# The openings of the first attention: tokens by way of a DRAM copy, another order of SP's transfers, and banks in one turn

## The reference, cut to what matters

```python
# L0: 32 query heads of 16, 8 key/value heads, post layer norm
q = x @ Wq + bq;  k = ctx @ Wk + bk;  v = ctx @ Wv + bv
attn = softmax(q k^T / sqrt(16) + mask)           # four query heads share one key head
x = layernorm(attn v @ Wo + bo + x) * gamma + beta
# L1: two attentions (16 heads of 128, pre layer norm, one learned key and value more) and an MLP
x = x + attention(layernorm(x), ctx; wq1 ...);  x = x + attention(layernorm(x), ctx; wq2 ...)
x = x + gelu(layernorm(x) @ w_fc1 + b_fc1) @ w_fc2 + b_fc2
```

## Time and profile before

| what | us |
|---|---|
| runs before (three) | 2495.45, 2500.95, 2508.18; median 2500.95 |
| the profiled execution, its own time | 2500.87 |
| its span, first to last instruction | 2499.0 |
| busy: PE / DVE / ACT / POOL | 2319.4 / 1397.6 / 996.5 / 786.4 |
| DMA | 248.60 MB, mean 99 GB/s |

### The profile page before, as it was taken

One profiled execution on the slowest core, in us unless ns is written; L12 is line 12 of the kernel. 1 busy time (PEld: TensorE's weight loads), 2 busy tenths in 40 slices (PEclk: granted clock), 3 DMA queues, 4 the chain that ended last, 5 costly groups with the idle time before them and its releaser, 6 DMA issues. The chain is left out here.

```text
span 2499.0 us, 36057 instructions
## 1 busy us (share of the span) xinstructions
PE 2319.4 (93%) x13176; PEld 2074.8 (83%) x13176; DVE 1397.6 (56%) x3138; ACT 996.5 (40%) x2191; POOL 786.4 (31%) x847
## 2 busy tenths in 40 slices
PE   6698899999999999998988979999999999999988
PEld 5576789998989999997776758898999899998976
DVE  4697544454565455456538965454545654455564
ACT  3596433242433333243128953243434333242420
POOL 4132322415141422414541332415141422415055
PEclk8899999999999999999998999999999999999999
DMA  8341223233323323234363213223332323233222
GB/s 254 100 133 44 85 86 110 81 89 119 97 83 95 94 86 110 81 89 138 118 191 101 76 39 101 85 85 119 94 96 86 94 86 110 81 91 117 81 71 80
DMA packets 136996, 248.60 MB, mean 99 GB/s; under 512 B 35663, under 2 KB 57295, under 8 KB 135799
## 3 DMA queue, kind: packets, MB, share of 16 engines
q1 hardware_dynamic: 93327, 123.54, 16.7%
q10 hardware_dynamic: 43496, 122.76, 16.0%
HBM read 221.35 MB, written 27.65 MB: 100 GB/s over the span
## 5 line engine op out<-in xcount | busy, mean ns | idle before, releaser
L622 POOL TENSOR_SCALAR wk_hi<-raw 128x512 fp32r<-128x512 f32 (+1 forms) x84 | 53.6, 638 | 905.4 <-DMA raw<-in_wk 751.1
L1325 ACT ACTIVATE probs<-scores,prm 112x376 f32<-112x376 f32 x256 | 147.0, 575 | 342.5 <-DVE prm L1682 342.4
L755 PE MATMUL pj_two<-ctx_hi,wk_hi 128*128 128x376 f32 x736 | 253.0, 344 | 10.6 <-POOL wk_lo L624 4.6
L756 PE MATMUL pj_two<-ctx_lo,wk_hi 128*128 128x376 f32 x736 | 248.3, 337 | 0.0
L757 PE MATMUL pj_two<-ctx_hi,wk_lo 128*128 128x376 f32 x736 | 247.6, 336 | 0.0
L1466 DVE TENSOR_TENSOR rr<-pj_two,rr 128x448 fp32r<-128x448 f32 (+2 forms) x200 | 132.8, 665 | 163.2 <-ACT rr L1102 163.1
L624 POOL TENSOR_TENSOR wb_lo<-raw,wb_hi 128x512 fp32r<-128x512 f32 x152 | 200.4, 1318 | 12.7
L1468 DVE SCALAR_TENSOR_TENSOR k_lo<-pj_two,cur,k_hi 128x375 fp32r<-128x375 f32 x172 | 104.4, 607 | 169.7 <-ACT k_hi L1104 169.7
L1104 ACT ACTIVATE k_hi<-pj_two,cur 128x375 fp32r<-128x375 f32 x172 | 98.6, 573 | 247.6 <-PE pj_two L757 242.7
L760 PE MATMUL tp_two<-ident,probs 112*126 112x112 f32 (+1 forms) x1152 | 163.8, 267 | 33.8 <-ACT probs L1245 18.2
L760 PEld LDWEIGHTS tp_two<-ident,probs 112*126 112x126 f32 (+1 forms) x1152 | 146.2, 160 | 56.3 <-ACT probs L1245 18.8
(11 more groups left out here) (246 smaller groups left out, 6640.1 us busy)
## 6 DMA issues: line engine op xcount, KB each, us to landing
nat<-nat_scratch ACTq DMA_DIRECT2D x256, 384.0 KB, 3.7
raw<-in_wq SPq DMA_DIRECT2D x72, 256.0 KB, 3.2
raw<-in_wo SPq DMA_DIRECT2D x72, 256.0 KB, 2.6
raw<-in_wk SPq DMA_DIRECT2D x64, 256.0 KB, 3.8
raw<-in_wv SPq DMA_DIRECT2D x64, 256.0 KB, 4.1
raw<-in_w SPq DMA_DIRECT2D x64, 256.0 KB, 2.9
nat_scratch<-rr ACTq DMA_DIRECT2D x7, 1536.0 KB, 6.8
qo<-queries_scratch SPq DMA_DIRECT2D x128, 56.0 KB, 2.4
```

The source lines that it names most:

```text
L622: nc.gpsimd.tensor_scalar(hi, src, 1.0, 0.0, ALU.mult, ALU.add).then_inc(split_hi, 1)
L755: nc.tensor.matmul(dst, l_hi, r_hi, start=first, stop=False)
L756: nc.tensor.matmul(dst, l_hi, r_lo, start=False, stop=False)
L1325: nc.scalar.activation(probs[0:L, h, 0:SK], scores[n % SCR][0:L, 0:SK], ACT.Exp, bias=neg_max[0:L, h:h + 1], accum_out=row_sum[0:L, h:h + ...
```

## The change

- **Tokens.** A DRAM scratch `x_copy` is new. SP copies each half's columns of `x_t` into it by one transfer (`copy_x`: the first half's ahead of all but the key weights, the second's in L0's attention), and loads them by two transfers of 448 KB into `pt_hi` and `pt_lo` (`x_came`, `load_x`). ScalarE casts the high part into `h_hi`, VectorE subtracts into `h_lo` (`split_x`). For the second half this is done in the last step of the first half's MLP.
- **Key weights.** GpSimd writes the scaled high part by one instruction; VectorE makes the low part from the raw slot and frees the slot (`wk0_rest`).
- **qo** is cleared first of all in the first half, and after the last chunk of `wq0` in the second.
- **Order of units.** The split of a context (`c`) and of the tokens (`x`) are named in the order; n3 comes after v0, and other units move (`pre_order`).
- **SP.** The stores of queries stand among the others in both openings, the queries of chunk 0 are loaded by 4 transfers in place of 16, the loads of bias rows and the zeros of `bx` move.
- **Banks.** `padded` goes; unit n of the whole program uses bank n modulo 3.

```diff
-def padded(n):
-    return -(-n // PJ) * PJ
+def pre_order(half):
     if half == 0:
-        order = "n0 n1 k0 k1 n2 n3 q0 k2 vt0 k3 vt1 v0 q1 vt2 v1 q2 vt3 v2 q3 v3"
+        order = "c0 n0 c1 k0 n1 k1 c2 n2 vt0 x0 k2 q0 vt1 v0 c3 n3 q1 vt2 v1 k3 q2 vt3 v2 q3 v3"
     else:
-        order = "k0 q0 k1 vt0 q1 vt1 v0 k2 q2 vt2 v1 k3 q3 vt3 v2 v3"
+        order = "k0 q0 k1 q1 vt0 q2 vt1 v0 k2 q3 vt2 v1 k3 vt3 v2 v3"
...
-    at["l0"], mid["l0"] = at["pre"] + padded(len(PRE[half])), mid["pre"] + len(PRE[half])
+    at["l0"], mid["l0"] = at["pre"] + len(PRE[half]), mid["pre"] + len(PRE[half])
...
+                def load_x(half):
+
+                    sp.wait_ge(x_copied, half * 16 + 16)
+                    for i in range(2):
+                        sp.dma_start(x_came[i], x_dram[2 * i * P:2 * (i + 1) * P, half * T:(half + 1) * T].rearrange(
+                            "(c p) n -> p c n", p=P)).then_inc(x_t_in, 16)
+
+                def copy_x(half):
+                    cols = slice(half * T, (half + 1) * T)
+                    sp.dma_start(x_dram[:, cols], x_t[:, cols]).then_inc(x_copied, 16)
...
+                if hf == 0:
+                    copy_x(0)
                 load_q0(base + RAW_Q0, 0)
-                for c in range(DC - 1):
-                    load_x(c)
+                load_v0(0)
+                if hf == 0:
+                    load_x(0)
+                load_v0(1)
                 if hf == 0:
                     store_keys0(0, *pre_split("k", 0))
-                load_x(DC - 1)
-                if hf == 0:
                     sp.dma_start(rows8_dram[0], bias_v).then_inc(rows8_in, 16)
                     sp.dma_start(rows8_dram[1], bv).then_inc(rows8_in, 16)
                     store_keys0(1, *pre_split("k", 1))
+                    load_q0(base + RAW_Q, 1)
+                    load_keys0(0, 0)
+                    load_keys0(0, 1)
+
+                    sp.wait_ge(pj_free, pre_freed("n", 2, SC - 1) + PJ)
+                    load_mask()
+                    load_q0(base + RAW_Q + 1, 2)
+                    store_keys0(2, *pre_split("k", 2))
+                    store_queries0(0, *pre_split("q", 0))
+                    load_q0(base + RAW_Q + 2, 3)
+                    load_queries0(0, 0)
+                    load_keys0(0, 2)
+                    sp.wait_ge(rows8_in, 32)
...
+                    store_queries0(1, *pre_split("q", 1))
+                    store_keys0(3, *pre_split("k", 3))
+                    store_queries0(2, *pre_split("q", 2))
+                    load_keys0(0, 3)
+                    store_queries0(3, *pre_split("q", 3))
+                else:
+                    for c in range(1, C0):
+                        load_q0(base + RAW_Q + c - 1, c)
                     store_keys0(0, *pre_split("k", 0))
...
+                            copy_x(1)
...
+                    sp.wait_ge(pj_ready, gpj + unit["r", HB - 1, DC - 1] + 1)
+                    sp.wait_ge(ex_in, 16 + NG * HB * 48)
+                    sp.sem_inc(sp_passed, 1)
+                    load_x(1)
...
+                    nc.gpsimd.tensor_scalar(hi, src, SCALE0, 0.0, ALU.mult, ALU.add).then_inc(split_hi, 1)
...
+            def split_x(half):
+                act.wait_ge(x_t_in, (half + 1) * 32)
+                for i in range(2):
+                    nc.scalar.activation(h_hi[:, 2 * i:2 * i + 2, :], x_came[i], ACT.Copy).then_inc(tok_hi, 1)
...
+            def wk0_rest(half):
+
+                for i in range(2):
+                    src, hi, lo = wk0_pieces(i)
+                    dve.wait_ge(split_hi, half * RAW_H + i + 1)
+                    nc.vector.scalar_tensor_tensor(lo, src, SCALE0, hi.bitcast(F32), ALU.mult,
+                                                   ALU.subtract).then_inc(w_ready["k"], 2)
+                    dve.wait_ge(w_ready["k"], half * WK_H * DC + 2 * (i + 1))
+                    dve.sem_inc(raw_free[i], 1)
...
-                    move(k_hi[:, h, 0:S], pj[unit % PJ][:, 0:S], pj_ready, gpj + unit + 1,
+                    move(k_hi[:, h, 0:S], pj[(gpj + unit) % PJ][:, 0:S], pj_ready, gpj + unit + 1,
```

More of the change, by code:

```diff
@@ L70, in pre_units, with banked @@
     return names
+def banked(names):
+    return [n for n in names if n[0] not in ("c", "x")]
+def pre_units(half):
+    return banked(pre_order(half))
 def pre_mids(half):
     names, held = [], None
-    for name in pre_units(half):
+    for name in pre_order(half):
         if name[0] == "vt" and name[1] > 0:
@@ L789, in out_part @@
                         ready(h)
-                    last = three(pj[unit % PJ][0:L, :],
+                    last = three(pj[(base + unit) % PJ][0:L, :],
                                  [s[:, h, b * L:(b + 1) * L] for s in src],
```

219 lines of the change are left out of this document (108 added, 111 removed).

## The result

The changed kernel takes 2487.42 us (median of 7 runs, 2484.52 to 2488.33), the kernel before 2504.41 us beside it (7 runs). The ratio is 0.9935, interval 0.9921 to 0.9949: faster by 0.65%. The profiled spans are 2499.0 and 2484.3 us, so 14.7 us are gone where 30 were forecast (17.0 by the two medians); the time lies inside the range.

What follows compares the result with a forecast made beforehand. SP's in-order queue, sending the last query stores late, was taken to set the end of both L0 openings; 18 us in the first plus 12 in the second off 2500.87 gave 2471 us, range 2452 to 2490.

Steps and rivals of the forecast that it cites:

- B: Rival: everything behind the token copy in SP's queue waits for its landing; first gate at 80 us, total 2486; chance 0.12.
- raw slots that hold the second opening: Second opening, rival's other condition: raw slots hold it, so it gains 6 us, with 9 in the first: 2486 us.
- the sum for SP's chain: First opening: 21.5 + 25.6 stores + 9 loads + 4 waits + 13.5 ACT traffic = 73.6, overlap to 71; 18 us gained.
- TensorE's chain: First opening: units walked to about 55 us against 69 before; last query store leaves at 57 to 58, ScalarE goes at 63.
- waits for landed key and query stores 4: First opening, SP's queue: waits for landed key and query stores take 4 us.
- The sixteen query loads: First opening, chunk 0's queries: sixteen loads took 14 us, four take 2.5 to 3.6, so 10 to 12 us go.
- Second opening: ScalarE let go at 1311 instead of 1323.3: 12 us gained, bounds 18 and 6.
- The half rate of the stores: Stores alone reach 0.52 DMA share, 190 GB/s; the change leaves this; full rate would put the first opening some 12 us earlier.
- Tokens: First opening: copy lands at about 14 us, casts 0.9 and subtractions 1.1 us each, tokens split at 29.5 instead of 37.5.
- The second half's copy: Tokens copied at about 135 us beside the context's copy in L0's attention; no price given to the copy there.
- MLP's cover: Before the MLP: token load delays w1 by up to 6 us, covered by 8.9 us before its first use.
- Banks: Unit boundaries: one turn of banks gives 0, bounds 0 and 0.4 us at each of about 20.

Runs made afterwards that it cites:

- experiment 7: Changed kernel with each half's tokens copied twice in DRAM, the load waiting for both copies; ratio to the kernel before 0.9963.
- (4): Changed kernel with chunk 0's queries loaded by 16 transfers again instead of 4, in both openings; ratio to the kernel before 0.9971.
- experiment 2: Changed kernel with each key and query store over 128 consecutive scratch rows, so attention works on mixed heads; ratio to the kernel before 0.9859.
- version 10: Changed kernel with scratch laid out for transfers over uniform rows, each key part stored once and read twice; 2462.11 us, ratio to the kernel before 0.9846.
- version 13: Changed kernel with the second half's token copy moved behind the first group's loads of the layer after; 2483.83 us, ratio to the kernel before 0.9940.
- 14: version 10 with the second half's token copy moved behind the first group's loads of the layer after; 2461.66 us, ratio to the kernel before 0.9852.
- (8): Kernel before with only the banks of pj in one unbroken turn; ratio to the kernel before 0.9990.
- version 2: The same run as experiment 2: changed kernel with key and query stores over 128 consecutive scratch rows; ratio to the kernel before 0.9859.
- 1: Changed kernel with the last query stores ahead of the wait for keys, or of the third batch's key stores; ratio to the kernel before 0.9928.
- version 6: Changed kernel with the load of query weight chunk 1 ahead of the first key stores, first opening; ratio to the kernel before 0.9956.
- version 12: version 10 with the last query stores earlier and query weight chunk 1 loaded ahead of the first key stores; 2463.09 us, ratio 0.9844.

## Why the prediction was right and wrong, point by point

- **What bounds, and where: right.** At both gates ScalarE waits for the last query stores, which SP's queue sends late, and the sign and the range held. Of the rivals none is it. B's 2486 is near the time, and its 80 us is where the gate came, but by chance: the copy that it blamed costs nothing there (experiment 7). Its other condition, raw slots that hold the second opening, came in part (below).
- **The step that failed: the sum for SP's chain, in its terms for landing.** In the first opening the forecast has 49.5 us from the second load of wv (21.5) to the gate (71). Stores and loads are 25.6 + 9 = 34.6 of it; SP issued, or waited for data of its own core, for 34.1, so these are right as a sum, if the ACT queue's traffic is counted with the waits. Its "waits for landed key and query stores 4" and the 13.5 for the ACT queue's traffic, less the 2.6 that were taken to overlap, are 14.9; SP's waits on landed stores measured **21.6**. The landing of the last query store has no term in this sum, though TensorE's chain has 5 us for it (57 to 58, then 63); it measured **5.3**. Together these are 12.0 us too few, of which an earlier start (18.8) gives 2.7 back. The kernel before already had 13.1 us of waits on landed stores, in the view of waits from which I had taken the rows of other engines only the earlier trace rows.
- **Stores were too dear, loads too cheap.** SP issued the stores in 21.2 us of the timeline, 25.6 forecast; loads and all else are the other 12.9 of the 34.1 us, 9 forecast. The sixteen query loads were priced 10 to 12 us above the four; 4.2 were measured in the first opening and 2.2 in the second (4). The sum also speaks of twelve key and six query stores still to come, but all 16 and 8 were, and its 25.6 has them all.
- **Second opening: 4.9 us instead of 12, by the same kind of term.** From the output's store to the gate 38.6 us were forecast and 46.0 measured. SP's first key store went 10.4 us behind the output's store (7.1 forecast), as the raw slots came free late: 3.3 us. From there to the last query store's leaving it was 26.8 us (27.6 forecast). That store's landing took **8.9 us**, where 2 were forecast and 2 more came in by taking 1311 for 1309. SP waited 8.8 us on landed keys, but 6.5 of them stand behind the last query store and do not hold the gate. The half clock that was to go with TensorE's wait was there again: 4.28 us of waiting for chunk 1 of wq (2 forecast), and a granted clock of 0.50 at 1274 to 1278 us.
- **What half-wide stores have to do with it.** With all stores wide (2) the waits on landed stores are 16.9 us, near the 14.9, the last landing is 2.7, issuing is 6.4 us shorter, and the second opening takes 36.4 us in all. So the two terms were missed in good part because stores at half rate take long to land.
- **TensorE's chain: wrong by 13 us.** It was walked to 55 us with weights on time; its first scores came at 68.4. Chunk 1 of wq was split 13 us after its load was issued at 32.5, chunk 3 also 13 us after (48.8 to 61.7). I had priced stores on SP's queue and on the bytes, but not on the loads that share the engines with them. With wide stores the first scores come at 59.6, in version 10 at 57.9, so some 3 to 5 us of it are not from the width.
- **The half rate of the stores was read and then not followed far enough.** The prediction gave the full rate "some 12 us" in the first opening; experiment 2 measured 14.5 there. The number was right, but it stood apart, as a fact about stores, when it also bears on the failed terms and on late weights. One row was misread on the way: at 20 to 22 us no key or query store had been issued yet (the first is at 27.85), so the 0.97 and 408 GB/s there are the rate of loads and of the ACT queue's store, not of these stores with others beside them.
- **Tokens: right in kind.** No wait for `h_lo` but 0.67 us; casts of 0.94 and subtractions of 1.09 us as sized; the split at 33.1 to 36.3 instead of 29.5, because it stands behind vt0, which was late. What the new way of the tokens gave by itself is not shown.
- **The second half's copy: missed, and without weight in the sum.** It was named and given no price. It cost 3.5 us in L0's attention (13, 14), where the cover that I had in mind, the attention's work, is two batches of loads deep; by the MLP the lead was back at 8.6.
- **MLP's cover: right.** The last w1 part was ready at 1156.8 and its first use at 1160.97, still set by the layer norm: 4.2 of the 8.9 us are left.
- **Banks: right**, nothing (8).

## What to carry to other kernels

Before summing a queue's transfers, list its waits on its own landed stores in the kernel before, and the time from the last store's leaving the queue to its landing: both are terms of the sum. When a stage view shows the DMA engines at half their time while an opening waits for its stores, change the layout so that each store runs over many uniform rows before touching the order; here the change and the new layout together gave 38 us, the change alone 16, and with the layout the places tried in the order stopped mattering. A copy "beside" other work can hold the loads behind it on the same queue: here four of them took 8.5 us to issue, and TensorE stood for 2.8.

## What the runs showed of the hardware

- Where stores of keys and queries are alone, the share of the DMA engines is 0.53 and the rate 199 GB/s with 8 in the first dimension, and 1.03 and 377 GB/s with 128 rows (6 us of the second openings, changed kernel and version 2).
- Half-wide stores make the loads behind them late in two ways. The queue is held up: the second four key stores take SP 6.25 us to issue, 4.42 when wide, and two in their place 1.64 in version 10, so chunk 1 of wq is issued at 32.5, 27.0 and 23.9 us. And it lands later: it is split 13.0, 9.0 and 10.4 us after its issue, at 45.5, 36.0 and 34.3.
- A copy from DRAM to DRAM of 0.92 MB landed in 6.0 us among the context's loads, but not behind a 3 MB copy: the median of the two token copies is 11.1 us from issue to landing (transfers by line, after), and 6.6 where the second goes alone (version 13).

```profile
x_copy<-in_x_t SPq DMA_DIRECT2D x2, 896.0 KB, 11.1
```

- The same wait differs between executions by more than some edits are worth: for the second part of wv none (1, 2, 13) to 10.6 us (4), although nothing ahead of that load was changed, for chunk 1 of wq in the second opening 2.6 to 7.1. From the gate to the output's store it was 1180.8 to 1190.5 us, 1189.0 in version 6 and 1187.1 in version 12, where no edit touches that stretch (1183.6 in the changed kernel, 1182.9 in version 10); part of it is the wait behind the copies (4.43 us in version 6), the rest I can't name. So one profile doesn't tell a gain of 3 us in the whole, and the readings above rest on the openings and on single waits.
